# Two VectorE instructions over many tiles, made in pieces of two tiles each

## What is computed

```python
edge_index = stack([src, dst])
x = layernorm(x + L0(edge_index, edge_type_16, x))   # two relational convolutions, 16 relations
x = layernorm(x + L1(x, edge_index))                 # attention, 8 heads of 16
x = layernorm(x + L2(x, src, dst, edge_type_8))      # relational, 8 relations, batch norm
x = layernorm(x + L3(x, edge_index))                 # two mean aggregations

# L1, the attention layer
h = (x @ lin_w.T).reshape(n, 8, 16)
logits = leaky_relu((h * att_src).sum(-1)[src] + (h * att_dst).sum(-1)[dst], 0.2)
e = exp(logits - segment_max(logits, dst)[dst])
alpha = e / segment_sum(e, dst)[dst]
agg = segment_sum(h[src] * alpha[:, :, None], dst)
out = layernorm((agg + gat_bias) @ proj_w.T + proj_b)

# L3, each of its two convolutions
mean = segment_sum(x[src], dst) / max(degree, 1)
out = mean @ W_l.T + b + x @ W_r.T
```

## Time and profile before

| what | value |
|---|---|
| time, median of 3 runs | 5924.92 us |
| lowest and highest of them | 5918.19 and 5926.52 us |
| span of the profiled execution (its own time is given by its span alone) | 5914.8 us |
| instructions | 110,361 |
| busy: PE, DVE, ACT, POOL | 4223.3, 2686.0, 1772.9, 4151.1 us |
| mean granted TensorE clock | 0.836 of full speed |
| first and last start of L806 (attention gathers) | 2448.4 and 3554.1 us |
| first and last start of L846 in near round c | 3668.9 and 4739.6 us |

### The profile page before, as it was taken

One profiled execution on the slowest core, in us unless ns is written; L12 is line 12 of the kernel. 1 busy time (PEld: TensorE's weight loads), 2 busy tenths in 40 slices (PEclk: granted clock), 3 DMA queues, 4 the chain that ended last, 5 costly groups with the idle time before them and its releaser, 6 DMA issues. The chain is left out here.

```text
span 5914.8 us, 110361 instructions
## 1 busy us (share of the span) xinstructions
PE 4223.3 (71%) x25432; PEld 3507.0 (59%) x25433; DVE 2686.0 (45%) x10126; ACT 1772.9 (30%) x5020; POOL 4151.1 (70%) x4271
## 2 busy tenths in 40 slices
PE   5688878878777777466666667666666657877786
PEld 3577777767777776455555555555555545555554
DVE  8743434343333332465656566445544552224222
ACT  0122222222222222344444445444444430002001
POOL 3177777757777776477777773777777757776777
PEclk6699999999999999565656567888888889888898
DMA  3266656542211111233333332233232344444443
GB/s 84 59 171 157 155 160 159 154 129 53 52 52 52 52 53 50 65 83 83 83 83 83 83 80 57 87 99 99 87 99 87 99 134 142 136 146 126 147 136 106
DMA packets 383068, 594.88 MB, mean 101 GB/s; under 512 B 120483, under 2 KB 289988, under 8 KB 372420
## 3 DMA queue, kind: packets, MB, share of 16 engines
q0 software_dynamic: 133120, 276.30, 17.9%
q1 hardware_dynamic: 245156, 310.79, 17.8%
q10 hardware_dynamic: 4128, 1.75, 0.1%
HBM read 519.07 MB, written 69.42 MB: 99 GB/s over the span
## 5 line engine op out<-in xcount | busy, mean ns | idle before, releaser
L1418 PE MATMUL PS<-ROOM 128*128 128x128 f32 x8320 | 1046.0, 283 | 130.7 <-ACT ROOM L1019 99.3
L1418 PEld LDWEIGHTS PS<-ROOM 128*128 128x128 f32 x8320 | 987.0, 196 | 190.0 <-ACT ROOM L1019 108.1
L846 POOL DMA_INDIRECT GB<-table,IDX x832 | 805.5, 968 | 316.9 <-issue 252.9
L1019 ACT COPY ROOM<-PS 128x512 f32<-128x512 f32 x1040 | 609.3, 586 | 1020.8 <-PE PS L1432 1019.4
L846 POOL DMA_INDIRECT GB<-in_x,IDX x416 | 404.8, 973 | 294.7 <-ACT IDX L993 158.0
L1432 PE MATMUL PS<-OH,GB 128*128 128x256 f32 (+1 forms) x1664 | 367.8, 384 | 242.3 <-DMA GB<-table,IDX 189.0
L2083 DVE TENSOR_TENSOR ROOM<-ROOM,PS 128x128 f32 x312 | 89.7, 287 | 988.7 <-PE PS L1442 981.2
L806 POOL DMA_INDIRECT GB<-table_gat,IDX x416 | 430.3, 1034 | 127.6 <-issue 126.5
L818 POOL DMA_INDIRECT GB<-table,IDX x416 | 395.5, 951 | 173.2 <-issue 125.6
L806 POOL DMA_INDIRECT H<-table_gat,IDX x416 | 423.1, 1017 | 126.8 <-issue 125.2
L846 POOL DMA_INDIRECT ROOM<-table,IDX x416 | 409.0, 983 | 126.8 <-issue 125.6
(11 more groups left out here) (415 smaller groups left out, 7964.1 us busy)
## 6 DMA issues: line engine op xcount, KB each, us to landing
H<-one_over SPq DMA_DIRECT2D x416, 128.0 KB
ROOM<-one_over SPq DMA_DIRECT2D x416, 128.0 KB
neighbours<-ROOM SPq DMA_DIRECT2D x26, 1700.0 KB
ROOM<-neighbours SPq DMA_DIRECT2D x26, 1700.0 KB
PACK<-neighbours SPq DMA_DIRECT2D x26, 1700.0 KB
ROOM<-local_row SPq DMA_DIRECT2D x104, 256.0 KB, 3.4
GB<-table,IDX POOLq DMA_INDIRECT x1248
ROOM<-table,IDX POOLq DMA_INDIRECT x832
```

Source lines behind the costliest of these rows:

```text
L846: pool.indirect_dma_start(out=r.rows[c][:, j * P:(j + 1) * P], out_offset=None, in_=r.dram[:, :], in_offset=bass.IndirectOffsetOnAxis(ap=I ...
L1019: act.copy(to.rearrange("p r (j d) -> p r j d", j=r.per), of.rearrange("p (j d r) -> p r j d", j=r.per, d=NEAR))\
L1418: ins = nc.tensor.matmul(PS[:, 4, 0:P], r.near[1 - b][:, t * P:(t + 1) * P], r.weights[:, t * P:(t + 1) * P], start=t == 0, stop=t == r.re ...
```

## The change

Both instructions are issued in pieces of `PIECE = 2` tiles. The product of the gathered rows and the weights, one instruction over 8 tiles, becomes four over 2 tiles (256 columns) each; the semaphore step is put on the last. The comparison for the low one-hots, one instruction over 5 or 6 tiles, becomes three: 2, 2 and 1 or 2, 2 and 2 tiles. The data, the results and the order of everything else are as they were.

```diff
+PIECE = 2
...
                 tiles = TILES_OF[c]
                 m = len(tiles)
-                dve.tensor_tensor(HOT_LO[c % 2][:, 0:m, :], mid(iota_h[:, 0:P], m),
-                                  last(lo_col[:, bass.ds(d * (CYCLE * G) + tiles[0], m)], P), ALU.is_equal)
+                for n in range(0, m, PIECE):
+                    w = min(PIECE, m - n)
+                    dve.tensor_tensor(HOT_LO[c % 2][:, n:n + w, :], mid(iota_h[:, 0:P], w),
+                                      last(lo_col[:, bass.ds(d * (CYCLE * G) + tiles[0] + n, w)], P), ALU.is_equal)
...
                 dve.tensor_tensor(own, own, last(start[:, bass.ds(k * G, G)], HEADS), ALU.mult).then_inc(soft_d, 1)
-                dve.tensor_tensor(MW[:, b, :, 0:P].rearrange("p j (h c) -> p j h c", c=HD),
-                                  gat_rows(c)[:, :, 0:P].rearrange("p j (h c) -> p j h c", c=HD),
-                                  MW[:, b, :, P:P + HEADS].unsqueeze(3).to_broadcast([P, G, HEADS, HD]), ALU.mult)                    .then_inc(soft_d, 1)
+                for j in range(0, G, PIECE):
+                    tiles = slice(j, j + PIECE)
+                    ins = dve.tensor_tensor(MW[:, b, tiles, 0:P].rearrange("p j (h c) -> p j h c", c=HD),
+                                            gat_rows(c)[:, tiles, 0:P].rearrange("p j (h c) -> p j h c", c=HD),
+                                            MW[:, b, tiles, P:P + HEADS].unsqueeze(3).to_broadcast([P, PIECE, HEADS, HD]), ALU.mult)
+                ins.then_inc(soft_d, 1)
```

## The result

| | before | after |
|---|---|---|
| median of the timed runs | 5925.72 us (4 runs, 5918.19 to 5930.62) | 5875.03 us (4 runs, 5872.8 to 5881.44) |
| span of the profiled execution | 5914.8 us | 5871.0 us |
| ratio of the times, 95% interval | | 0.992 (0.9908 to 0.9932) |

The kernel is 0.8% faster: 51 us by the medians, 43.8 us by the spans. The forecast was 5863 us, with a range of 5848 to 5893.

What follows compares the result with a forecast made beforehand. GpSimd, issuing gathers one behind the other, was taken to bound both rounds. Gains of 43 us (product) and 19 us (low one-hots) cut the span from 5914.8 to 5852.8; adding 10.1 gave 5863 us, range 5848 to 5893.

Steps and rivals of the forecast that it cites:

- What holds the gathers: Both rounds: a gather asks 0.12 us after its start and, when VectorE holds what it needs, waits for that instruction's end.
- The product's gain: Attention round, L2245 in four pieces: 55.1 - 8.7 - 3 = 43 us gained, ends 26 and 52.
- The cover of VectorE: Attention round: VectorE's 188.1 us of waiting for gathered rows hides the time that the product's pieces add.
- the 13 us that were to stay: Attention round: cost of the other long gathers, by L2295, L2186 and L1962, expected to remain.
- The 23 us: Attention round: VectorE time added by the product's four pieces, 0.22 us a batch over 104 batches.
- the rival that ends slower: VectorE becomes the bound, the loop's late turns never being caught up: 5960 us; both slower cases 0.06 together.
- The low one-hots' gain: Third near round, L1956 in three pieces: 25.9 us of gather delay falls to 5 plus 2; gain 19 us, ends 12 and 22.
- the missed hand-over: Early requests not let in at an instruction's end; small shares put down: 3 us at the product, 2 at the low one-hots.
- pieces pass the hold to each other: Rival: GpSimd isn't let in between pieces, at product and low one-hots: 5953 us; both slower cases 0.06 together.
- The sum: Whole kernel: 43 + 19 = 62 us off the span, 5914.8 to 5852.8 us.
- The 10.1 us between span and median: Whole kernel: the median of the runs, 5924.9, lies this far above the span; added to reach 5863 us.

Runs made afterwards that it cites:

- The pair of added instructions: Product in 2s, low one-hots whole, plus an unread 1,024-column tensor_reduce or two-SBUF-input tensor_tensor behind each product; ratios 1.0006 and 1.0015 to the kernel before.
- the breaks in the product: Product in pieces of two tiles, VectorE waiting for its own last piece between them, low one-hots whole; 5920.9 us, ratio 0.9989 to the kernel before.
- the added instruction: Product in 2s, low one-hots whole, plus an unread one-input tensor_reduce of 1,024 columns behind each product; 5932.01 us, ratio 1.0006 to the kernel before.
- the kernel with fours and breaks: Changed kernel with the product in two instructions of four tiles and VectorE waiting for its own piece between low one-hot pieces; 5862.83 us, ratio 0.9902 to the kernel before.

## Why the prediction was right, and where it was not

**What holds the gathers: right.** A gather asks 0.12 us after its start and waits for the end of a tensor_tensor with both inputs in SBUF. The pair of added instructions shows it (none of 65 held by the reduce, all of 54 by the tensor_tensor).

**The product's gain: right, and nearer than it should have been.** 43 us were forecast (26 to 52), and the attention round's delay fell by 45.6. The forecast put down what the product costs gathers at 55.1 us, and that fell by 38 to 17: some 65 gathers wait for the end of one piece, 11.4 us together, where 8.7 were put; and five pass through several, 5.8 us, where 3 were put. The other 7 us came from elsewhere. In the kernel before, 49 gathers asked during the scans L2290 and L2295 and lost 7.5 us; in the changed kernel 4 do and lose 0.2, while with the low one-hots alone in pieces the 7.7 us stay. They were among the 13 us that were to stay, so that this part is luck.

**The cover of VectorE: right here, and thinner than the text made it.** The 23 us cost nothing. But the 188.1 us were to fall by 0.63 us a batch, to some 122 us, and fell to 96: the 24 us of other idle time, which is a part of VectorE's own turn, had no place in the working. 106 us more (the breaks in the product) or 118 (the added instruction) made VectorE the bound and lengthened the round by 24.5 and 34.4 us. This is the rival that ends slower, and by these two (106 - 24.5 and 118 - 34.4) it decides from some 80 us of further VectorE time in this round.

**The low one-hots' gain: the step that failed.** 19 us were forecast, with 12 as the low end, and nothing came. The step was: "at most 3 x 0.23 us per set against 1.25, x 0.115, x 78 = 5 us, and 2 us for early requests that miss". The 5 us were near (some 30 gathers that were let in at the end of their own piece or the next cost 6 us); the 2 us were 19. The text had seen the missed hand-over the earlier trace rows and given it a small share because L1989 has none; but behind each instruction of L1989 stands the short reading of its accumulator, and between the pieces nothing stands. Whether that is the difference was not tried, and the trace of the kernel before has a case against it. In near round b the eight instructions of L1992, of 256 columns too, follow each other with nothing between them, each starting 0.07 to 0.09 us before the last one's end. 85 gathers were held in one that had another behind it, and 84 of them were let in at its end, as here, where one asks at 2300.78:

```profile
2300.19 2.67 DVE L1992 TENSOR_SCALAR H<-iota_w,key,PACK 128x256 f32<-128x256 f32 x8 [0.89 <-DVEq L2062]
2300.66 1.08 POOL L846 DMA_INDIRECT H<-table,IDX  x1 [0.30 <-issue]
```

So a run without gaps is needed for a gather to be shut out, as far as these traces show, but isn't enough; what else it takes stays open. The rival "pieces pass the hold to each other" was true for some of the gathers at this line and for few at the other. In the 26 turns of the loop it hit 15 gathers.

**The sum.** The span was to fall by 62 us and fell by 43.8: the low one-hots fell short by 21 us, and the attention round gave 3 more than forecast. The 10.1 us between span and median were not a constant: the median lies 4.0 us above the span after, and in the profiled execution whose time is known (5872.8 us) 1.8 us are outside of its span. So some 8 of the 10.1 us were that the profiled execution before was one of the quicker ones. These two errors, 18 and 6 us, went against each other, and that the time came within 12 us of the forecast is in part luck.

**Rules of the Trainium skill.** The page "SBUF — State Buffer", section "Who interferes with whom", says that a tensor_reduce on trn2 never contends with GpSimd, and this case agrees (0 of 65 gathers were held). It infers that a tensor_tensor doesn't stall the generation of descriptors; here 54 of 54 gathers were held to its end. The measurement decides. The advice of at least 512 elements an instruction ("VectorE: DVE Perf Modes", section on the TRN2 errata) turned out to do no harm, for another reason: pieces of 512 columns gain as much as those of 256 (0.9919 and 0.9924) and those of 128 less (0.9938), and the delays of the gathers (22.2, 23.5 and 37.0 us) account for that, with no need of the fixed cost.

## What to carry to other kernels

Where a row of gathers sets the time, look at each long one beside the other engine's timeline: a long VectorE tensor_tensor with two SBUF inputs holds them to its end, and cutting the product in two gave all that finer pieces gave. Read afterwards whether gathers wait through several pieces. Where they do, a wait of the engine for its own piece puts a gap between two of them, at 0.12 to 0.22 us a gap and more behind the last; this paid in the near round, where VectorE is busy for half of the time, and not in the product. And count the cover of the helping engine by its waits for the bound one, with its waits for third engines as part of its own turn: at 64% busy, VectorE had 96 us left in a round of 1,061 us, and using them up took nearly all or all of the gain (0.9989 and 1.0006 in place of 0.9924).

## What the runs showed of the hardware

- Back-to-back VectorE instructions can shut a gather out for their whole chain, for 1.5 us in the near round (a gather of 2.42 us) and 1.7 us in the attention round (2.64 us) of the changed kernel: no hand-over at five ends in a row. Where VectorE paused behind the piece there was one every time: 76 gathers asked in a low piece of the kernel with fours and breaks, 30 took no longer for it, and the other 46 were let in at that piece's end, 41 of them with a pause behind it. Without a pause many were let in too: some 65 of 70 at the product of the changed kernel. The 15 long ones of its near round had asked 0.146 to 0.20 us after the start of an instruction, but 14 others that asked in the same stretch were let in at that instruction's end, and in the kernel with the low one-hots alone five long ones had asked 0.34 us after the start of one piece, within 0.02 us of the next one's start. What decides was not settled. But a gap always ended the wait: in the first four rounds of all 14 traces 5,218 gathers took over 1.0 us, and only three of them waited past idle time of VectorE, each 0.05 us of it and near 53 us, at the start of the first round.
- A gather that was shut out into the key tiles ends 0.98 us after the end of one of them (the first in 13 cases, the second in one), and 0.69 us after the end of the next, but not 0.82 us after any; this repeats to 0.01 us in all 14. Why is open.
- VectorE's waits for its own instruction can cost more behind the last one than between them: three in the product cost 0.36 us between the pieces (0.12 each) and 0.65 us ahead of the scan that follows, 0.58 of them idle time. The same wait between two low pieces cost 0.22 us. Why they differ is open.
- Not all one-input instructions let gathers pass. The tensor_reduce in fp32 does; the one-input key tile (tensor_scalar, fp16 to bf16, 600 columns, 0.39 us), L2189 (tensor_scalar, bf16) and, in the kernel before, L1992 (tensor_scalar, fp32, 256 columns: 120 of 134) hold gathers as the tensor_tensor with two inputs in SBUF does. The tensor_tensor with an input in PSUM (L2083) held none of 70.
- The near round, with the same instructions in it, had 2 to 13 long gathers and took 1,064 to 1,072 us over seven kernels. How much of that is due to what went before it, and how much is scatter, isn't shown: the changed kernel's two profiles differ by 4.7 us in that round.
